# The adjacency's 32x32 transposes on VectorE and three normalisations on GpSimd, in a graph network with routed experts

## What is computed

```
def gnn(x, adj, W1, b1, W3, b3, Wf, bf):
    h = relu(adj @ (x @ W1) + b1)
    h = relu(adj @ (h @ W3) + b3)
    return tanh(h @ Wf + bf)

x = x + gnn(layernorm(x), adj, ...)
x = x + ffn(layernorm(x), ...)       # 8 experts, hidden size 1024, the best 2 for each row
```

## Time and profile before

| | us |
|---|---|
| median of 3 runs | 667.93 |
| lowest | 666.84 |
| profiled execution | 665.48 |
| its span, first to last instruction | 663.4 |

### The profile page before, as it was taken

The page is one execution under the profiler, slowest core; times in us unless marked ns, Lnnn a source line. Parts: engine busy times, 40 slices in busy tenths (PEclk is TensorE's granted clock), DMA queues, the critical chain, the costliest instruction groups (busy, mean ns, idle before and its releaser), DMA issues.

```text
span 663.4 us, 11473 instructions
## 1 busy us (share of the span) xinstructions
PE 612.1 (92%) x3472; PEld 519.3 (78%) x3473; DVE 340.9 (51%) x752; ACT 312.9 (47%) x589; POOL 146.6 (22%) x143
## 2 busy tenths in 40 slices
PE   3999999999999989989888999999999999999970
PEld 3888888887868666768776898888888888888860
DVE  4875444464555775645744333337333736377620
ACT  2667474765545474355522332345234526356520
POOL 3000000000000505036445222331333134223222
PEclk9999999999999999999989999999999999999985
DMA  8993000020002763422163111216211715376312
GB/s 306 377 381 151 1 0 1 1 96 0 1 32 64 166 184 102 131 65 44 13 205 82 18 27 33 34 24 213 32 32 19 218 32 150 87 216 165 79 30 33
DMA packets 35315, 63.74 MB, mean 96 GB/s; under 512 B 5018, under 2 KB 27164, under 8 KB 33724
## 3 DMA queue, kind: packets, MB, share of 16 engines
q1 hardware_dynamic: 26620, 52.32, 23.6%
q0 software_dynamic: 8224, 10.53, 9.5%
q10 hardware_dynamic: 432, 0.39, 0.2%
HBM read 54.02 MB, written 10.26 MB: 97 GB/s over the span
## 4 chain that ended last, share of the span: by engine, by line
PE 84%; DVE 5%; ACT 4%; issue 3%; DMA 1%; another core or an unknown queue 1%; POOL 0%; POOLq 0%; ACTq 0%; DVEq 0%
PE bank L1566 42%; PE bank L1435 8%; PE bank L1437 8%; PE bank L1436 8%; PE bank L1411 4%; PE bank L1613 4%; PE bank L1462 3%; PE bank L1396 2%; PE bank L1448 2%; PE bank L1559 1%; DVE ring L926 1%; PE bank L1486 1%; PE bank L1460 1%; DVE ew L1258 1%; PE bank L1637 1%
## 5 line engine op out<-in xcount | busy, mean ns | idle before, releaser
L1566 PE MATMUL bank<-ew,xeT 128*128 128x512 f32 x840 | 203.8, 397 | 4.0 <-DVE ew L1258 2.1
L1566 PEld LDWEIGHTS bank<-ew,xeT 128*128 128x128 f32 x840 | 155.8, 189 | 36.2 <-issue 4.1
L926 DVE TENSOR_TENSOR ring<-adj_s,ring 128x512 fp32r<-128x512 f32 x128 | 87.5, 688 | 77.8 <-ACT adj_s L607 42.3
L1435 PE MATMUL bank<-ring,Z 128*128 128x512 f32 x256 | 110.0, 430 | 6.3 <-DVE ring L926 4.7
L1566 PE MATMUL bank<-ew,heT 128*128 128x256 f32 x840 | 110.6, 289 | 4.7 <-issue 2.3
L1566 PEld LDWEIGHTS bank<-ew,heT 128*128 128x128 f32 x840 | 104.3, 194 | 6.2 <-issue 6.0
L1437 PE MATMUL bank<-ring,Z 128*128 128x512 f32 x256 | 100.9, 394 | 0.0
L1436 PE MATMUL bank<-ring,Z 128*128 128x512 f32 x256 | 100.2, 391 | 0.0
L523 POOL DMA_INDIRECT out<-y_st,idx_st x29 | 45.5, 1570 | 190.7 <-ACT y_st L759 168.8
L490 POOL DMA_INDIRECT slot_rows<-val,route x32 | 34.8, 1087 | 218.6 <-issue 217.7
L765 ACT ACTIVATE sil<-bank 128x512 f32<-128x512 f32 x58 | 34.7, 599 | 86.1 <-PE bank L1566 86.1
(11 more groups left out here) (183 smaller groups left out, 653.4 us busy)
## 6 DMA issues: line engine op xcount, KB each, us to landing
w_raw<-in_L_ffn_W SPq DMA_DIRECT2D x24, 1024.0 KB, 5.6
adj_s<-in_adj SPq DMA_DIRECT2D x12, 1024.0 KB, 6.3
adj_s<-in_adj SPq DMA_DIRECT2D x8, 512.0 KB, 6.9
x_in<-in_x SPq DMA_DIRECT2D x4, 512.0 KB, 7.9
x_res<-in_x SPq DMA_DIRECT2D x4, 512.0 KB, 3.6
out<-x SPq DMA_DIRECT2D x4, 512.0 KB, 3.4
ffn_in_rows<-x_res SPq DMA_DIRECT2D x4, 512.0 KB
xg<-ffn_in_rows,idx POOLq DMA_INDIRECT x39
```

The source lines that it names most:

```text
L926: nc.vector.tensor_tensor(lo, src, hi, ALU.subtract).then_inc(s_lo, 1)
L1435: nc.tensor.matmul(a, zh, hi, start=(jb == 0), stop=False)
L1566: last = nc.tensor.matmul(out_ap, stat[:, sl, k, :], w_at(k, wl), start=(k == k0 and sl == wl == 0), stop=(k == k1 - 1 and sl == 1))
```

## The change

Adj is no longer transposed by TensorE. SP loads it in 16 quarters n = 4c + k of 512 rows by 512 columns. A quarter comes in four transfers, one for each quadrant q of 32 partitions; partition 32q + i receives, for each of 16 values r, the 128 adjacent columns that belong to q of row 32r + i of the chunk, a run of 512 bytes. VectorE then transposes the quarter in place in 32x32 squares (`turn`, four pieces of 128x512), and after this a block jb lies in 16 runs of 32 columns inside its quarter. Within a chunk and within x's groups, nodes are permuted to fit: x is loaded by four transfers per group, and `hidden1` writes its output back in the plain order.

The turns are dealt over VectorE's list: turns 0 to 5 ahead of the first subtraction (AHEAD_TURN = 6), then turn s + 6 after each subtraction of layer 1. ScalarE makes only the high part of a block, from SBUF, and takes over `z2_out` from VectorE. For x's groups 1 to 3, VectorE makes statistics and the reciprocal, and GpSimd the four normalisations; group 0 stays on VectorE. The small weights are now issued ahead of quarter 8, and quarter 12 waits for Z.

```diff
+            x_nodes = x.rearrange("(g q b j) d -> g q j b d", g=NC, q=CT, b=CT)
+            adj_quads = adj.rearrange("(c r i) (k q m) -> c k q i r m", c=NC, i=SQ, k=NC, q=CT)
+
             def x_load(g):
-                sp.dma_start(x_in[:, CT * g:CT * (g + 1), :], xv[:, CT * g:CT * (g + 1), :]).then_inc(s_x[g], 16)
+                for q in range(CT):
+                    sp.dma_start(x_in[SQ * q:SQ * (q + 1), CT * g:CT * (g + 1), :], x_nodes[g, q]).then_inc(s_x[g], 16)
+
+            def adj_load(n):
+                c, k = n // NC, n % NC
+                if n >= NC:
+                    sp.wait_ge(s_adj[n % NC], QUADS * c)
+                for q in range(CT):
+                    rows = adj_s[SQ * q:SQ * (q + 1), n, :].rearrange("p (r m) -> p r m", m=P)
+                    sp.dma_start(rows, adj_quads[c, k, q]).then_inc(s_adj[n % NC], 16)
...
+            for n in range(NC):
+                adj_load(n)
+                if n + 1 < NC:
+                    x_load(n + 1)
+            for n in range(NC, NC * NC):
+                if n == 2 * NC:
                     weight_load(1, W3, s_w)
...
-                if t == NT - 2:
+                if n == NC * (NC - 1):
                     sp.wait_ge(s_zp, NT)
+                adj_load(n)
...
@@ GpSimd @@
+            def x_norm(g):
+                pool.wait_ge(s_rstd, g)
+                for i in range(CT):
+                    v = x_in[:, CT * g + i, :]
+                    last = nc.gpsimd.tensor_scalar(v, v, mv[:, i, 0:1], rstd[:, i:i + 1], ALU.subtract, ALU.mult)
+                last.then_inc(s_xn, 1)
...
@@ ScalarE, hi_of_block @@
                 if layer == 0:
-                    act.wait_ge(s_tp, s + 1)
-                    src = tp[s % 2][:, :].rearrange("p (i n) -> p i n", i=CT)
-                    nc.scalar.copy(dst, src).then_inc(s_hi, 1)
-                    nc.scalar.copy(blk, src).then_inc(s_adjT, 1)
-                else:
-                    nc.scalar.copy(dst, blk).then_inc(s_hi, 1)
+                    act.wait_ge(s_turn, CT * (s // CT + 1))
+                nc.scalar.copy(ring_part(s, 0), block_of(c, jb)).then_inc(s_hi, 1)
...
@@ ScalarE @@
+            def z2_out(t):
+                act.wait_ge(s_z2p, t + 1)
+                nc.scalar.copy(z2[:, t, :], sm[t % 2][:, 0:D]).then_inc(s_z2, 1)
...
@@ VectorE, x_norm @@
                 if part == 1:
+                    if g >= 2:
+                        dve.wait_ge(s_xn, g)
                     spread()
-                if part == 2:
+                if part == 2 and g > 0:
+                    dve.wait_ge(s_sqrt, g + 1)
+                    nc.vector.reciprocal(rstd[:, :], std[:, :]).then_inc(s_rstd, 1)
+                if part == 2 and g == 0:
                     roots(g + 1)
...
@@ VectorE @@
+            def turn(p):
+                n = p // CT
+                dve.wait_ge(s_adj[n % NC], QUADS * (n // NC + 1))
+                v = adj_s[:, n, CW * (p % CT):CW * (p % CT + 1)]
+                nc.vector.transpose(v, v).then_inc(s_turn, 1)
...
+            turn(0)
             x_T_lo(0)
+            turn(1)
             x_T_lo(1)
+            turn(2)
+            turn(3)
             z1_lo(0)
+            for p in range(CT, AHEAD_TURN):
+                turn(p)
             for s in range(2 * S1):
                 lo_of_block(s)
+                if s + AHEAD_TURN < S1:
+                    turn(s + AHEAD_TURN)
...
@@ TensorE @@
-                if s + 2 < S1:
-                    transpose_block(s + 2)
                 product(s)
```

More of the change, by code:

```diff
@@ L35, in gnn_and_routed_ffn @@
     HW = 512
+    SQ = 32
+    QUADS = 16 * CT
+    AHEAD_TURN = 6
     RING = 3
@@ L207, in gnn_and_routed_ffn @@
         s_w = sem("s_weights_in")
-        s_adj0 = [sem(f"s_adj_row{t}") for t in range(CT)]
-        s_adj = [sem("s_adj_even"), sem("s_adj_odd")]
+        s_adj = [sem(f"s_adj_quarter{n}") for n in range(NC)]
         s_pool = sem("s_pool_own")
@@ L215, in gnn_and_routed_ffn @@
         s_xn = sem("s_xn")
+        s_rstd = sem("s_x_rstd")
         s_xtp = sem("s_xT_psum")
@@ L288, in static, with block_of, ring_part, by_block @@
             return isinstance(v, int)
+        def block_of(c, jb):
+            return adj_s[:, CT * c + jb // CT, :].rearrange("p (r b j) -> p r b j", b=CT, j=SQ)[:, :, jb % CT, :]
+        def ring_part(s, lo):
+            return ring[:, s % RING, lo, :].rearrange("p (r j) -> p r j", j=SQ)
+        def by_block(v):
+            return v.rearrange("p (b q j) -> p q b j", b=CT, q=CT)
         def expert_load(sp, e, n):
@@ L532, in main_add @@
                 add_rows(j + EARLY, idx_st[:, j % YR, :])
+            def x_norm(g):
[4 more added lines that the diff above has]
+                last.then_inc(s_xn, 1)
+            for g in range(1, NC):
+                x_norm(g)
             pool.wait_ge(s_none, 16)
@@ L710, in _ @@
                     hidden1(s // NT - 1, jb - 1)
+                if NT <= s < S1 + NT and jb in (5, 6):
+                    z2_out(CT * (s // NT - 1) + 2 * jb - 10)
+                    z2_out(CT * (s // NT - 1) + 2 * jb - 9)
                 if jb == 1 and s > S1 + NT:
@@ L918, in lo_of_block @@
                 layer, c, jb = s // S1, s % S1 // NT, s % NT
[L919 to L926, removed]
+                dve.wait_ge(s_hi, s + 1)
+                nc.vector.tensor_tensor(ring_part(s, 1), block_of(c, jb), ring_part(s, 0).bitcast(F32),
+                                        ALU.subtract).then_inc(s_lo, 1)
             def z_lo(t):
@@ L1398, in z1_rows @@
                 last.then_inc(s_zp, 1)
[L1400 to L1404, removed]
-                if c >= 1 and jb == 0:
-                    for par in range(2):
-                        pe.wait_ge(s_adj[par], 16 * (CT * c // 2))
-                if s >= 2:
-                    pe.wait_ge(s_adjT, s - 1)
-                for i in range(CT):
-                    last = nc.tensor.transpose(tp[s % 2][:, i * P:(i + 1) * P],
-                                               adj_s[:, CT * c + i, jb * P:(jb + 1) * P], ident[:, :])
-                last.then_inc(s_tp, 1)
             def product(s):
```

40 lines of the change are left out of this document (4 added, 36 removed).

## The result

The changed kernel takes 671.9 us (median of 14 runs) against 666.6 us for the kernel before beside it (14 runs). The ratio is 1.007, with a 95% interval of 1.0051 to 1.0089: 0.7% slower, where I had forecast 1.5% faster. The one run of before at 889 us is left out of the ratio. The profiled execution has a span of 669.9 us, 6.5 more than before.

A forecast was written before the change was run, and what follows sets the result against it. TensorE was taken to bound the first layer, with VectorE becoming the bound in part of chunk 0. The terms +5.0 + 2.2 + 3.9 − 21.0 = −9.9 us took 667.9 to 658.0 us, range 645 to 677.

The forecast's parts named there:

- What bounds the kernel now: First layer: TensorE never idles and sets the time; VectorE is four fifths full in chunk 0.
- Part 1, chunks 1 to 3: Without TensorE's transposes, 0.47 us per step, these chunks fall from 32.1 to 24.6 us each; net −21.0 us.
- the 1.5 us charged for all three chunks together: Chunks 1 to 3: allowance for the hidden layer's low part in one go and ScalarE's new copies.
- Part 2, the turn: VectorE's 64 transposes of 128x512 cost 0.61 us each, bounds 0.42 and 1.22; covered in chunks 1 and 2.
- rival 2: On VectorE's queue from the prologue on, each turn costs 1.22 us as a double pass; 679 us; chance 9%.
- Part 3, GpSimd's operation: Chunk 0: four normalisations per group at 0.6 us each, bounds 0.45 and 1.14, stall each of three groups 1.0 us.
- Part 4, the loads: Adjacency transfers into 32 partitions run at 205 GB/s, bounds 187 and 282; the first product starts at 21.9 us, +5.0.
- The wait for the weights, +3.9: Chunk 0, step 11: VectorE arrives at 54.3 us and waits for the small weights until 58.2.
- Part 5: Shorter block reads and hidden-layer output by blocks cost nothing; second layer and experts keep their work and only shift.
- the term +2.2: Chunk 0 takes 42.7 us against 40.5, VectorE being the bound; the 0.47 saved per step is used up there.
- rival 3: Transfers run below 187 GB/s because jumping reads are slow; at 150 GB/s, 678 us; chance 11%.
- rival 4: Transfers run at 282 GB/s, but GpSimd stands behind VectorE each time, 6.3 us more; 656 us; chance 6%.

The follow-up runs named there:

- experiment 1: The changed kernel with the normalisation of x's groups 1 to 3 back on VectorE; 663.2 us, 0.9969 of the kernel before.
- experiment 2: The kernel before with only the normalisation of x's groups 1 to 3 moved to GpSimd; 679.8 us, 1.0217 of the kernel before.
- experiment 5: The changed kernel with useless matmuls on TensorE, 20 ahead of the first product and 14 ahead of each wait for GpSimd; 666.4 us, 1.0007 of the kernel before.
- experiment 3: The changed kernel with transfers for partitions 64 to 127 issued from ScalarE's queue instead of SP's; 671.4 us, 1.009 of the kernel before.

## Why the prediction was wrong, by its own steps

**What bounds the kernel now**: right. Taking work off TensorE paid at the predicted pitch wherever nothing else was late (1.36 us per step).

**Part 1, chunks 1 to 3**: predicted −21.0, measured −13.6. The mechanism was right, and about 1.0 of the 7.4 us is a slip in the sum: TensorE transposes two steps ahead, so chunk 3 of before had transposes in 14 steps, not in 16, and took 30.9 us, not 32.1. The term that was mis-sized is the 1.5 us charged for all three chunks together: it is 2.2 in each of chunks 1 and 2 and 3.6 in chunk 3. I had named both causes, the hidden layer in one go and ScalarE's new copies, and summed queues over a whole chunk. My reading is that the ring of three blocks covers about one short step of lateness, so a burst counts by its own length. Before, a step of 1.83 us had swallowed the same bursts: its steps 16 to 19 took 7.31 us, which is 4 × 1.83. The same copies cost 0.6 us in steps 64 to 79, which I had left out.

**Part 2, the turn**: 0.61 predicted, mean 701 ns and the following operation 0.62 to 0.63 us later. Right, and rival 2 is out. "The saving of 0.47 per step is used up there" was right for chunk 0 as well: even with the normalisation on VectorE it takes 42.9 us against 42.3.

**Part 3, GpSimd's operation**: this step failed. I took 0.6 us from rows of a one-column TENSOR_SCALAR and of a MEMSET, and bounded it above at 1.14. It takes 1.25. Four of them are 5 us; VectorE stood idle 4.1 to 4.3 us in each of three groups, not 1.0. In the first group, from the reciprocal at 24.43 on, the four take 5.2 us instead of 2.4, the transposes, copies and hand-overs 1.4 instead of 0.75, and VectorE's own work beside them is 2.5 instead of 2.2. The low part of x that VectorE waits for has no cover. A MEMSET reads nothing, and one column shows no cost per column: the rows had nothing from which to take a rate for an operation that reads, computes and writes, and the range should have said so. Experiments 1 and 2 put 9 and 14 us on this edit (in experiment 1 the weights' wait took some of its place).

**The clock**: in no step, and 4 to 5 of chunk 0's 16.0 us (experiment 5). I had idle time of TensorE in the forecast and priced it at its own length. Each idle stretch was followed by matmuls at 1.2 GHz, 0.63 us instead of 0.40.

**Part 4, the loads**: 205 GB/s predicted. Behind 20 us it was 217, but from 2.2 to 20 us, the stretch that sets the first product, 230 (4.09 MB in 17.8 us). So the side to lean to was right, and the rate was 12% too low where it counted: quarter 1 was there at 18.1 us (VectorE's two turns start on it then, after 3.5 us of waiting for the transfer), 1.7 sooner than worked out, and the first product came at 20.0, not at 21.9. The wait for the weights, +3.9, was right as a mechanism (4.4 in experiment 1) and hidden in the changed kernel itself, because VectorE came there at 68.2 us; in experiment 1 they had landed at 58.0.

**Part 5**: layer 2 unchanged, 94.92 and 94.93 us for steps 80 to 123. Right.

**The slip**: with 42.3 us for chunk 0 of before, the term +2.2 would have been +0.4 and the forecast 656.2; it hides nothing of the error, and points the other way. From the forecast of −9.9 to the measured +6.5 are 16.4 us: −1.8 for the first product, +9.9 for chunk 0 with the weights' wait (6.1 predicted, 16.0 measured), +7.4 for chunks 1 to 3, +0.8 behind them. The range of 645 to 677 held the 671.9 only because it reached to rivals 2 and 3, which did not happen. Slow GpSimd operations were in rival 4 alone, tied there to quick transfers and at 6%.

## What to carry to other kernels

Moving work to an idle engine is priced by that engine's own time for the operation on that shape; where no row of the trace shows it with data read and written, keep it off any path that another engine's list waits for in order. (Whether statistics taken a few steps earlier would have hidden GpSimd's 5 us, no run shows.) When a wait on TensorE is added, price the work behind it at half the clock as well. When the bound engine gets quicker, bursts on its feeders that were hidden in its longer step come out, and they are counted step by step, against the depth of the ring.

## What the runs showed of the hardware

GpSimd's TENSOR_SCALAR with two per-partition operands takes 1.25 us for 128x256 float32 (1.22 in the median), against VectorE's 0.33 from start to start in the same kernel before (four in 1.30). VectorE's 32x32 transposes of 128x512 float32 take 701 ns.

Transfers into 32 partitions at a time give 217 to 222 GB/s with runs of 512 or of 2048 bytes, and into 128 partitions 277 with runs of 512. Two queues that fill two halves of the partitions at once give 295 (20:30 of experiment 3). ScalarE was held for 5.9 us by a pair of issues made while seven earlier transfers of its queue had not landed, and for 0.9 by a pair made with none before it (at 36.7 us of the same run).

Behind its four idle stretches in the changed kernel (4.6, 3.1 and twice 3.95 us) TensorE ran at 1.2 GHz, 0.63 us for a product instead of 0.40; with matmuls put into these stretches it stayed at 2.4.
